# One GELU per MLP block on ScalarE, and the rounded half written by a VectorE copy

## The reference

```
x1 = residual + (out @ wo + bo)
n2 = _ln(x1, ln2_g, ln2_b)
mlp = jax.nn.gelu(n2 @ w1 + b1, approximate=False) @ w2 + b2
return x1 + mlp
```

## Time and profile before

| | us |
|---|---|
| median of 3 runs | 2246.26 (2245.17 to 2248.73) |
| the profiled execution | 2243.45 |
| its span, first to last instruction | 2241.6 |
| PE busy | 2211.5 |
| ACT busy | 1934.4 |
| DVE busy | 1836.9 |
| POOL busy | 1544.8 |

### The profile page before, as it was taken

One profiled execution on the slowest core, in us unless ns is written; L12 is line 12 of the kernel. 1 busy time (PEld: TensorE's weight loads), 2 busy tenths in 40 slices (PEclk: granted clock), 3 DMA queues, 4 the chain that ended last, 5 costly groups with the idle time before them and its releaser, 6 DMA issues. The chain is left out here.

```text
span 2241.6 us, 78295 instructions
## 1 busy us (share of the span) xinstructions
PE 2211.5 (99%) x29492; PEld 2120.6 (95%) x29492; DVE 1836.9 (82%) x6993; ACT 1934.4 (86%) x6478; POOL 1544.8 (69%) x1613
## 2 busy tenths in 40 slices
PE   7999999999999999999999999999999999999998
PEld 6999999999999999999999999999999999999988
DVE  5888888888888888888888888888888888877885
ACT  6788988988888889889889888888898898888876
POOL 6776767766776777676677677767776776766752
PEclk8999999999999999999999999999999999999999
DMA  4101011011011011010110110110110101101000
GB/s 133 33 30 33 23 33 40 28 33 39 21 40 40 21 40 35 26 40 28 33 40 28 33 40 21 39 40 21 40 34 27 40 28 33 40 28 40 26 11 18
DMA packets 95781, 76.88 MB, mean 34 GB/s; under 512 B 9648, under 2 KB 95152, under 8 KB 95408
## 3 DMA queue, kind: packets, MB, share of 16 engines
q1 hardware_dynamic: 93632, 71.73, 10.5%
q10 hardware_dynamic: 1776, 0.14, 0.1%
HBM read 55.06 MB, written 16.78 MB: 32 GB/s over the span
## 5 line engine op out<-in xcount | busy, mean ns | idle before, releaser
L881 POOL TENSOR_TENSOR probs<-probs,rinv 128x512 f32<-128x512 f32 x512 | 562.3, 1119 | 363.6 <-DVE rinv L737 363.6
L599 ACT ACTIVATE probs<-probs,negmax 128x128 f32<-128x128 f32 x2048 | 794.6, 394 | 7.8 <-DVE negmax L723 4.0
L599 ACT ACTIVATION_READ_ACCUMULATOR probs<-probs,negmax 128x1 f32 x2048 | 394.1, 192 | 0.0
L809 DVE TENSOR_TENSOR hT_low<-hidden,hT_high 128x512 fp32r<-128x512 f32 x256 | 267.7, 1047 | 42.0 <-ACT hT_high L640 41.9
L533 PE MATMUL ring_ps<-w_high,hT_high 128*128 128x256 f32 x1024 | 294.4, 288 | 1.2 <-DVE hT_low L809 1.2
L395 PE MATMUL ring_ps<-inT_C_high,w_high 128*128 128x256 f32 x1024 | 289.6, 283 | 0.6 <-DVE inT_C_low L694 0.6
L533 PE MATMUL ring_ps<-w_low,hT_high 128*128 128x256 f32 x1024 | 283.5, 277 | 0.0
L533 PE MATMUL ring_ps<-w_high,hT_low 128*128 128x256 f32 x1024 | 283.4, 277 | 0.0
L395 PE MATMUL ring_ps<-inT_C_low,w_high 128*128 128x256 f32 x1024 | 283.3, 277 | 0.0
L395 PE MATMUL ring_ps<-inT_C_high,w_low 128*128 128x256 f32 x1024 | 283.1, 276 | 0.0
L469 PE MATMUL ring_ps<-ident,probs 128*128 128x128 f32 x2048 | 269.6, 276 | 0.2
(11 more groups left out here) (150 smaller groups left out, 7085.2 us busy)
## 6 DMA issues: line engine op xcount, KB each, us to landing
xT_sb<-in_xT_dram SPq DMA_DIRECT2D x64, 256.0 KB, 2.8
x_sb<-in_x_dram SPq DMA_DIRECT2D x64, 256.0 KB, 3.1
out_dram<-x SPq DMA_DIRECT2D x128, 128.0 KB, 1.8
adj_B<-in_adj_dram SPq DMA_DIRECT2D x64, 128.0 KB, 2.2
adj_A<-in_adj_dram SPq DMA_DIRECT2D x64, 128.0 KB, 2.5
probsT_B<-in_L_gnn_w_dram SPq DMA_DIRECT2D x1, 1024.0 KB, 8.6
qT_B<-in_L_gnn_Wq_dram SPq DMA_DIRECT2D x1, 256.0 KB, 4.7
kT_B<-in_L_gnn_Wk_dram SPq DMA_DIRECT2D x1, 256.0 KB, 5.1
```

What stands on the lines that cost most here:

```text
L599: e = act.activation(probs[:, u, h, :], probs[:, u, h, :], ACT.Exp, bias=negmax[:, u, h:h + 1], scale=-1.0, accum_out=sums[:, u, h:h + 1])
L809: dve.tensor_tensor(hT[1][:, 2 * f:2 * f + 2, :], hidden[:, f % 2, :, :], hT[0][:, 2 * f:2 * f + 2, :], ALU.subtract).then_inc(s_h_low, 1)
L881: pool.tensor_tensor(probs[:, u, hs, :], probs[:, u, hs, :], rinv[:, u, hs].unsqueeze(2).to_broadcast([P, HR, P]), ALU.mult).then_inc(s_pr ...
```

## The change

ACT evaluates GELU once for each quarter, into `hidden` alone. The rounded half is written by a new DVE copy `hidden` to `hT[0]` in the step `low`, ahead of the subtraction that was there, with a semaphore `s_h_high` between the two. The wait on `d1` (only in the pairs of the first and last turns and the first steady ones) goes from ACT to DVE with the write that it guards.

```
-                if g and (name, g) in table.loose:
-                    act.wait_ge(s_full["d1"], g)
-                for dst in (hidden[:, f % 2, :, :], hT[0][:, 2 * f:2 * f + 2, :]):
-                    for i in range(2):
-                        e = act.activation(dst[:, i, :], ring(name, g)[:, i * T:(i + 1) * T], ACT.Gelu,
-                                           bias=b1_col[:, 2 * f + i:2 * f + i + 1])
+                for i in range(2):
+                    e = act.activation(hidden[:, f % 2, i, :], ring(name, g)[:, i * T:(i + 1) * T], ACT.Gelu,
+                                       bias=b1_col[:, 2 * f + i:2 * f + i + 1])
                 e.then_inc(s_out[name], 1)
...
             def low(name, g, f):
                 dve.wait_ge(s_out[f"u{f}"], g + 1)
+                if g and (name, g) in table.loose:
+                    dve.wait_ge(s_full["d1"], g)
+                dve.tensor_copy(hT[0][:, 2 * f:2 * f + 2, :], hidden[:, f % 2, :, :]).then_inc(s_h_high, 1)
+                dve.wait_ge(s_h_high, table.nth[name, g])
                 dve.tensor_tensor(hT[1][:, 2 * f:2 * f + 2, :], hidden[:, f % 2, :, :], hT[0][:, 2 * f:2 * f + 2, :],
                                   ALU.subtract).then_inc(s_h_low, 1)
```

More of the change, by code:

```diff
@@ L299, in build @@
         s_x1b, s_x2b = sem("s_x1b"), sem("s_x2b")
-        s_h_low = sem("s_h_low")
+        s_h_high, s_h_low = sem("s_h_high"), sem("s_h_low")
         def ring(name, g):
```

## The result

The changed kernel takes 2340.36 us (median of 4 runs, 2337.45 to 2341.16) against 2247.06 (4 runs): ratio 1.0417, 95% interval 1.0404 to 1.0429. It is 93 us slower. 2327 was predicted, and the measured time lies at the upper end of the forecast's own part of the range (2297 to 2342). The profiled executions give 2340.45 - 2243.45 = 97.0 us.

The account below looks back on a forecast made before the run. PE was taken to bound the kernel, with nx only 0.1 us early at tB. 60 turns of 1.35 us make 81 us on 2243.45, 2324.5, plus 2.8 for the median: about 2327 us; range 2272 to 2366.

Parts of the forecast that it names:

- PE bounds, `tB` and `nx` are the weak place: A steady turn is PE's own 34.11 us; nx is finished only 0.1 us before PE's transpose tB reads it.
- ACT's saving is worth nothing by itself in the steady part: 512 GELUs leave ACT, 229.0 us, but PE doesn't wait for ACT in a steady turn, so no gain by itself.
- The price of a copy: Each added DVE copy in the low steps takes 0.50 us, between bounds of 0.402 and 0.682.
- The lower bound: With copies of 0.40 us: lag about 1.0 at c3, stall 0.9 a turn, 54 us, 2300.
- The gap to the subtraction: The semaphore between DVE's copy and the subtraction adds 0.06 us each time.
- DVE and POOL take turns: They exclude each other for whole instructions; lags at c0, c1, c2, c3 become 0.06, 0.62, 0.82, 1.39 us.
- the rival of the lost lock: At c2 POOL's L881 starts before the copy: another 0.9 us, 2.2 a turn, 2378 us; chance 0.07.
- From `c3` to `nx` at the old distance: Minima, vB and nx follow c3 as before; PE stands about 1.3 us at tB, 1.35 with POOL's mask step.
- 60 turns of 1.35: Some 60 of 64 turns each lose 1.35 us at tB, 81 us in all.
- The little-slower rival: Old waits for POOL swallow copies at c0 and c2; c1 and c3 cost 0.5 us a turn, 2276; chance 0.13.
- No change: Copies hidden in holes at c1 and c3, lag at nx at most 0.1 us, time 2246 us; chance 0.05.
- faster: In the last 8 pairs PE waits for ACT's GELUs, each worth 0.7 us: 5.6 us, 2241; chance 0.04.

Follow-up runs that it names:

- e2: Changed kernel without the DVE copy, one GELU kept, rounded half filled once with a constant: 2237.4 us, ratio 0.9960 to the kernel before.
- e1: Kernel before with both GELUs kept and a same-size DVE copy to a spare tile added in each low step: 2365.7 us, ratio 1.0536.
- e5: Changed kernel with POOL's second-layer mask step cut to 8 of 128 columns per graph: 2306.0 us, ratio 1.0265 to the kernel before.
- e6: One GELU and the DVE copy only in quarters 0 and 2, quarters 1 and 3 as in the kernel before: 2262.1 us, ratio 1.0059.
- e7: One GELU and the DVE copy only in quarters 1 and 3, quarters 0 and 2 as in the kernel before: 2274.9 us, ratio 1.0117.
- e8: Changed kernel, steady turns reordered: moments y1 between c0 and c1, y2 ahead of tB, reciprocal rB0 right behind c0: 2289.0 us, ratio 1.0181.
- e9: e8 with vB and n1 moved ahead of the minima mA00 on DVE: 2301.7 us, ratio 1.0254 to the kernel before.
- e3: Changed kernel, steady turns reordered: moments y1 in y2's place, y2 ahead of tB, POOL's root i1 ahead of wB0: 2314.9 us, ratio 1.0308.

## Why the prediction was right

- *PE bounds, `tB` and `nx` are the weak place.* Shown: 56 waits of 1.38 us on average there, and 2.5 us in 5 waits of PE's loads for `c` steps in the whole run; a turn of 35.68 us against 35.46. `c3` came 1.07 us late, under the 1.58 that PE had to spare.
- *ACT's saving is worth nothing by itself in the steady part.* Shown by e2 (0.03 us a turn). That the change's saving matters once the copies are in was in the working (0.38 us at `c0`), and e1 measured 0.37. ACT's busy time is 1780 us and not near 1705: the 229.0 us of the earlier trace rows don't leave whole, since neighbours overlap on ACT (two pairs that last 0.94 and 0.96 us start 0.71 apart in the earlier trace rows). The rest of the difference was not taken apart, and no term of the sum hung on it.
- *The price of a copy* was too high: 0.43 us on average over all 256 (110.5 us of DVE), 0.38 to 0.42 in a steady turn, against 0.50. The working with 0.40 in place of 0.50 at `c1`, `c2` and `c3` gives lags of 0.52, 0.62 and 1.09, and 0.54, 0.62 and 1.07 were measured; so the copies' price accounts for that difference. (The lower bound's "about 1.0" at `c3` was thus 0.1 too low, and its 2300 should have been about 2306.) The gap to the subtraction was 0.03 us for the 0.06 taken, but the subtraction behind it took 0.69 for 0.66, which cancels. The estimate of 0.33 us worked out from the Trainium skill (VectorE: DVE Perf Modes, section on the TRN2 errata) is 0.05 to 0.09 below the copies of the steady turn; the measured price decides.
- *DVE and POOL take turns.* The lags at `c0` (0.08 for 0.06) and `c1` (0.54 for 0.62) were near; at `c2` DVE did get in first (0.62 for 0.82, the copies' price again), so the rival of the lost lock did not come true. The 0.9 us that the working gives POOL's first step there stands in no row (two undisturbed ones take 2.04 us in the trace of the kernel before, at 1025.26), but the lag came out as worked.
- *From `c3` to `nx` at the old distance* is the term that was mis-sized: 0.05 us was allowed for POOL's mask step, and it is 0.52 in the trace and 0.59 by e5. It more than makes up for the cheap copies, and so the lag at `nx` was 1.59 us where 1.40 to 1.45 was forecast. That the two errors, 0.3 too much for the copies and 0.5 too little here, nearly cancel is luck; the place and the way of the loss are not.
- *60 turns of 1.35* = 81 us: it was 50 of 1.56 = 78, and 19 us in the first and last pairs, where the ten others of the 60 were given 13.5. The cause of the larger loss there was not taken apart; that part of the 97 us is measured, not explained.
- *The little-slower rival* (copies free at `c0` and `c2`, 0.5 us a turn for `c1` and `c3`, 2276) came out for the halves apart: 0.14 us in e6, 0.50 and 2274.9 in e7. It did not for all four. *No change* and *faster* did not come out.

## What to carry to other kernels

Where one engine is busy all the time, price an edit on another by how long ahead of use each result behind it in that queue is finished, the smallest of these first; here 0.1 us at `nx` decided over 154 us of ACT time saved. An instruction added to VectorE also moves its neighbours against GpSimd's, and they may collide where they didn't (0.5 of 1.57 us a turn), so walk through both timelines as far as the result that is waited for. Copies in a schedule's holes were nearly free (e6: 0.14 us for two). Reordering gave back up to 1.03 of the 1.57 us (e8); the step beyond it, which made room for `nx`, made another result late (e9).

## What the runs showed of the hardware

A VectorE copy float32 to fp32r of 128x512 in SBUF took 0.37 to 0.42 us undisturbed (e1 and the changed kernel), 0.27 to 0.32 less than the subtraction of the same size behind it (0.69). Held up by GpSimd it ended 0.28 us behind GpSimd's instruction (e1: 1032.97 + 1.29 = 1034.26, the copy 1034.54; e3 above), where the subtraction ended 0.55 behind (`c0` in the earlier trace rows). That subtraction took 0.69 us behind the copy in the changed kernel and 0.66 without one in the kernel before, both undisturbed. GpSimd is held up as well: the power of two values (L891) took 1.16 us instead of 0.70 beside a subtraction. Not every step of POOL holds VectorE up alike: beside the one with an int32 input (L850) the two instructions of `nx` took 0.41 and 0.48 us in the kernel before, and beside the float32 one with two inputs (L854) the second took 0.89 us in the changed kernel.
